# A softmax over sixteen heads: maximum subtracted and rows summed on VectorE, one exponential for four heads on ScalarE

## What is computed

```
def heads(t):                                   # kc = 127 picked tokens, H = 16 heads, hd = 16
    return t.reshape(b, kc, H, hd).transpose(0, 2, 1, 3)
q = rope(heads(hn @ wq), pos_sel)
kk = rope(heads(hn @ wk), pos_sel)
v = heads(hn @ wv)
sc = jnp.einsum('bhqd,bhkd->bhqk', q, kk) / np.sqrt(hd).astype(np.float32)
sc = sc + m_sel[:, None]
a = jax.nn.softmax(sc, axis=-1)
o = jnp.einsum('bhqk,bhkd->bhqd', a, v).transpose(0, 2, 1, 3).reshape(b, kc, d) @ wo
```

## Time and profile before

| what | us |
|---|---|
| median of 3 runs (1541.77 to 1546.73) | 1543.58 |
| the profiled execution: its own time | 1547.94 |
| its span in the trace | 1546.2 |
| TensorE busy in it | 1406.5 (91%) |
| VectorE busy in it | 993.5 (64%) |
| ScalarE busy in it | 693.9 (45%) |

### The profile page before, as it was taken

One profiled execution on the slowest core, in us unless ns is written; L12 is line 12 of the kernel. 1 busy time (PEld: TensorE's weight loads), 2 busy tenths in 40 slices (PEclk: granted clock), 3 DMA queues, 4 the chain that ended last, 5 costly groups with the idle time before them and its releaser, 6 DMA issues.

```text
span 1546.2 us, 23272 instructions
## 1 busy us (share of the span) xinstructions
PE 1406.5 (91%) x8720; PEld 881.4 (57%) x8720; DVE 993.5 (64%) x2776; ACT 693.9 (45%) x1353; POOL 353.1 (23%) x417
## 2 busy tenths in 40 slices
PE   7999999999999999999999999999999999998444
PEld 2447645675457655576446764576555765466333
DVE  2426787377864787377973778647873679737672
ACT  4443544545354552635445353445526354452212
POOL 3004310332104301143103321043111430033210
PEclk9999999999999999999999999999999999999767
DMA  8000010020002001020010200020010200101010
GB/s 292 1 1 29 21 31 22 4 70 28 25 21 73 1 28 38 7 74 20 19 35 3 71 28 25 21 72 2 28 31 14 73 15 15 44 3 44 28 45 4
DMA packets 47536, 54.26 MB, mean 35 GB/s; under 512 B 7608, under 2 KB 42296, under 8 KB 47424
## 3 DMA queue, kind: packets, MB, share of 16 engines
q1 hardware_dynamic: 41408, 46.42, 9.2%
q0 software_dynamic: 6016, 6.35, 1.6%
HBM read 34.84 MB, written 17.87 MB: 34 GB/s over the span
## 4 chain that ended last, share of the span: by engine, by line
PE 81%; DVE 10%; issue 4%; ACT 4%; POOL 1%; DMA 1%; POOLq 0%; DVEq 0%; SPq 0%; ACTq 0%
PE ps L1521 38%; PE ps L1685 7%; PE ps L1595 4%; PE ps L1588 4%; PE ps L1636 3%; PE ps L1825 2%; PE ps L1648 2%; PE ps L1607 2%; PE ps L1835 2%; DVE xT L1192 2%; PE ps L1622 2%; PE ps L1790 2%; PE ps L1613 1%; PE ps L1509 1%; DVE EC L1373 1%
## 5 line engine op out<-in xcount | busy, mean ns | idle before, releaser
L1521 PE MATMUL ps<-xT,wc_s 128*128 128x512 f32 x512 | 232.6, 609 | 0.0
L1521 PE MATMUL ps<-xT,wb_s 128*128 128x512 f32 x512 | 230.9, 597 | 0.1
L1521 PEld LDWEIGHTS ps<-xT,wc_s 128*128 128x128 f32 x512 | 99.7, 198 | 116.5 <-issue 116.2
L1521 PEld LDWEIGHTS ps<-xT,wb_s 128*128 128x128 f32 x512 | 93.6, 190 | 108.4 <-issue 100.9
L1015 DVE SCALAR_TENSOR_TENSOR xT<-xc,cols_s,xT 128x512 f32<-128x512 f32 x192 | 134.9, 749 | 3.2 <-ACT xT L702 0.6
L1685 PE MATMUL ps<-CT,xT 128*128 128x256 f32 x512 | 114.5, 385 | 16.3 <-DVE xT L1192 16.3
L1685 PEld LDWEIGHTS ps<-CT,xT 128*128 128x128 f32 x512 | 98.1, 193 | 35.3 <-issue 21.9
L1521 PE MATMUL ps<-hT,wx_s 128*128 128x512 f32 x256 | 116.4, 604 | 1.3 <-ACT hT L667 1.3
L1521 PE MATMUL ps<-hT,wz_s 128*128 128x512 f32 x256 | 112.3, 592 | 0.0
L734 ACT ACTIVATE BT<-ps 128x512 f32<-128x512 f32 x64 | 37.9, 592 | 155.8 <-PE ps L1521 155.8
L775 ACT ACTIVATE XB<-ps 128x512 f32<-128x512 f32 x64 | 38.4, 599 | 153.6 <-PE ps L1607 153.6
(11 more groups left out here) (297 smaller groups left out, 2625.0 us busy)
## 6 DMA issues: line engine op xcount, KB each, us to landing
BT<-x SPq DMA_DIRECT2D x8, 1024.0 KB, 6.7
xr<-x SPq DMA_DIRECT2D x8, 1024.0 KB, 7.5
x_scratch<-xr SPq DMA_DIRECT2D x32, 256.0 KB, 2.1
out<-EC SPq DMA_DIRECT2D x32, 256.0 KB, 2.1
modrow<-mod_scratch SPq DMA_DIRECT2D x8, 512.0 KB, 4.5
w_s<-w SPq DMA_DIRECT2D x2, 1024.0 KB, 11.6
xT<-wmod SPq DMA_DIRECT2D x1, 1024.0 KB, 8.6
wb_s<-wbT SPq DMA_DIRECT2D x1, 1024.0 KB, 11.4
```

What stands on the lines that cost most here:

```text
L1521: ins = t_.matmul(bank[:, :], w[:, k, m * P:(m + 1) * P], rhs[:, k, half * HALF:(half + 1) * HALF], start=k == 0, stop=k == nk - 1)
```

## The change

The maximum is no longer negated and given to the exponential as a bias: VectorE subtracts it from the 508 columns of a group in place. The exponential is then one instruction for four heads, without bias and without the accumulator. The sums come from a reduction on VectorE at the head of each group in `ffn_probs`. `prob_ready` counts 4 in a batch where it counted 16, and the count of the chain R goes from 44 to 48 for the four new waits of VectorE on itself.

```
-CHAINS = {"A": 4, "V": 9, "D": 7, "S": 3, "G": 20, "R": 44}
+CHAINS = {"A": 4, "V": 9, "D": 7, "S": 3, "G": 20, "R": 48}
...
-        prob_ready = sig("prob_ready", FH)
+        prob_ready = sig("prob_ready", 4)
...
             def ffn_softmax(b):
-                for h in range(FH):
-                    if h % 4 == 0:
-                        act.wait_ge(mx_ready, at(mx_ready, b, h // 4 + 1))
-                    a.activation(scr[:, h, 0:NSEL], scr[:, h, 0:NSEL], ACT.Exp, bias=mx[:, h:h + 1],
-                                 accum_out=den[:, h:h + 1]).then_inc(prob_ready, 1)
+                for r in range(4):
+                    h = slice(4 * r, 4 * r + 4)
+                    act.wait_ge(mx_ready, at(mx_ready, b, r + 1))
+                    a.activation(scr[:, h, 0:NSEL], scr[:, h, 0:NSEL], ACT.Exp).then_inc(prob_ready, 1)
...
                     chR(dve, b, v.tensor_reduce(mx[:, h], scr[:, h, 0:NSEL], AX.X, ALU.max))
-                    v.tensor_scalar(mx[:, h], mx[:, h], -1.0, None, ALU.mult).then_inc(mx_ready, 1)
+                    v.tensor_tensor(scr[:, h, 0:NSEL], scr[:, h, 0:NSEL],
+                                    mx[:, h].unsqueeze(2).broadcast_to([P, 4, NSEL]), ALU.subtract
+                                    ).then_inc(mx_ready, 1)
...
             def ffn_probs(b):
                 for r in range(4):
                     h = slice(4 * r, 4 * r + 4)
-                    dve.wait_ge(prob_ready, at(prob_ready, b, 4 * r + 4))
+                    dve.wait_ge(prob_ready, at(prob_ready, b, r + 1))
+                    chR(dve, b, v.tensor_reduce(den[:, h], scr[:, h, 0:NSEL], AX.X, ALU.add))
                     chR(dve, b, v.reciprocal(den[:, h], den[:, h]))
                     v.tensor_tensor(scr[:, h, 0:NSEL], scr[:, h, 0:NSEL],
                                     den[:, h].unsqueeze(2).broadcast_to([P, 4, NSEL]), ALU.mult
                                     ).then_inc(pn_ready, 1)
```

## The result

The changed kernel takes 1587.27 us (median of 4, 1586.94 to 1589.48) against 1543.86 us of the kernel before in the same runs: a ratio of 1.0277, 95% interval 1.0258 to 1.0297. It is 43.4 us slower; the forecast was 1588.7. The profiled execution took 1587.46, its span is 1585.6.

The account below looks back on a forecast made before the run. TensorE, standing still at the transposes until VectorE ends `ffn_probs`, was taken as the bound. Seven passes of 4.8 + 0.8 us and a last of 4.9 + 1.0 gave 45.1 us, so 1588.7 against the median; range 1573 to 1600.

Parts of the forecast that it names:

- VectorE's queue is the path, and everything added to it arrives: TensorE waits for VectorE ahead of the transposes; each microsecond by which VectorE ends `ffn_probs` later arrives whole in the time.
- a first wait grown by less than 2.5 us: TensorE's wait at the transposes L1790, forecast near 5.9 us; growth below 2.5 us would show the forecast wrong.
- The three further waits: TensorE's waits for the later groups at the transposes, three in each pass, forecast at 0.4 to 0.9 us.
- The first reduction: First group of `ffn_probs`: the new reduction stands behind L1070, starts 0.2 us later, and the group is 2.8 us late.
- The transposes end 4.8 us later: TensorE at L1790: a group every 1.53 us, the last taking 1.19 at low clock, ending at 276.25, 4.8 us late.
- The clock, 0.8 us a pass: L1521 rows behind the transposes: half clock loses 1.95 us, less 1.15 already paid, so 0.8 us more a pass.
- The first rival: TensorE's broken work at the transposes brings the clock up, so the change costs only 26.4 us, 1570; chance 0.10.
- ScalarE at no cost and no gain: Softmax: sixteen exponentials become four, the last ending later at 266.5 but hidden by VectorE's own work; cost nothing.
- The last pass, 5.9 us: Pass without `decay_parts`: L1790 ends 4.9 us late, plus 1.0 us for low clock in the steps behind.
- The sum: Seven passes of 5.6 us, 39.2, plus 4.9 + 1.0: 45.1 us; 1593.0 against the profiled time, 1588.7 against the median.

Follow-up runs that it names:

- the filler ahead: Changed kernel with six extra 128x512 matmuls, results unused, ahead of TensorE's first wait at the transposes in each pass: 1594.20 us, ratio 1.0321.
- the piece put first: Changed kernel with the projection piece that follows the transposes put ahead of them in TensorE's queue: 1578.53 us, ratio 1.0216.
- the second execution of before: The kernel before, without any edit, profiled once more because its first profiled execution lay 4 us above the median: 1540.95 us.
- putting one block ahead of another: Kernel before with `ffn_probs` ahead of `decay_parts` in VectorE's queue: 1514.49 us against 1545.3, ratio 0.9809.

## Why the prediction was right, point by point

*VectorE's queue is the path, and everything added to it arrives.* Right. Subtraction: a group of 2.05 us was forecast and measured, `decay_parts` starts 2.08 us later (forecast 2.1). Normalisation: a period of 1.53 forecast, 1.52 measured.

One sign of a wrong forecast, a first wait grown by less than 2.5 us, came close: the wait grew from 3.05 to 5.57, by 2.52. The three further waits were forecast at 0.4 to 0.9 and are 0.34.

*The first reduction.* Forecast to put the first multiplication 2.8 us late; it is 2.5. The mis-sized step is the 0.2 us for which I let it stand behind the end of `decay_parts`: issued at 267.12, it ends 0.25 us after its predecessor L1069 does (267.50), so most of it was already under way.

*The transposes end 4.8 us later.* Measured 4.54 in the first pass and 4.64 on the average of seven; the group at low clock is 1.19 us, as forecast from the earlier trace rows. Over the seven passes this term is 1 us too large, by the step above.

*The clock, 0.8 us a pass.* Measured in this pair of profiles 0.32 (32.6 us for the seven projection pieces against 30.4). The mechanism is as forecast, and the size wasn't. Over full clock (3.37 us in the timeline) the piece costs 0.97 us more before and 1.29 after, on the average of seven passes, where I had 1.15 and 1.95. I had let the clock come back 4.0 to 6.1 us after the last group starts; it is back after 5.0 us in passes 2, 4 and 6, and after 2.6 in the others, where the piece takes 4.13 us instead of 5.35 and not the 4.8 to 5.9 of the forecast. Here lie 3.4 of the 5.5 us by which the sum exceeded the profiled execution (1593.0 against 1587.46). The first rival, by which the broken work brings the clock up, did not come about: in every pass of the changed kernel the clock is still 0.50 when the last group ends, and in two experiments broken work brings it down by itself (the filler ahead, the piece put first). That the idle stretch is what brings the clock down, as I had reasoned, is only part of it.

*ScalarE at no cost and no gain.* Right: 0.9997 for the fused exponential alone. The Trainium skill, page "VectorE: DVE Perf Modes", section on the TRN2 errata, advises large tiles so that a fixed cost of each instruction is spread. The traces agree: an exponential of 508 columns takes 627 ns, where four of 127 with bias took 1.28 us without the accumulator (the sums alone) and 1.54 with it. The rule says nothing on who waits.

*The last pass, 5.9 us.* Measured from the first scores to the end of the span, it is 6.7 us longer (47.7 against 41.0). The transposes are 4.8 late; the rest is the low clock in the steps behind, of which this timeline of the changed kernel shows the two that matter:

```profile
1552.37 1.19 PE L1792 MATMUL ps<-ident,EC 128*127 128x128 f32 x4 [0.34 <-DVE EC L1388]
...
1554.34 1.94 PE L1805 MATMUL ps<-EC,ftmp 127*32 127x128 f32 x32 [0.78 <-ACT EC L831]
...
1556.86 2.05 PE L1815 MATMUL ps<-fwo_s,ftmp 128*128 128x256 f32 x4 [0.58 <-ACT ftmp L837]
```

*The sum.* Pass by pass and from trace to trace: 34.7 in seven, 6.7 in the last, less 1.4 by which the first scores come earlier and 0.6 between passes, which is 39.4, the difference of the spans. The medians differ by 43.4, because the profiled execution of before lay 4 us above its median. The forecast of 1588.7 came so close to 1587.3 in part by luck: I carried over to the median a sum that is 5.5 us too large for the profiled pair. The extra of the clock is probably larger on the median than in this pair of traces, since the second execution of before, 7.0 us faster, pays less for it than the first. How much larger isn't settled by two profiles.

## What to carry to other kernels

An engine's saved time counts only where somebody waits for it: look for the wait before moving work, and move it away from the engine that carries the chain. Before splitting or fusing, ask for the order in that engine's queue: putting one block ahead of another here gave 31 us, the fused exponential alone nothing. And price what a slower feeder does to TensorE: here the work in pieces, and not the wait ahead of it alone, cost the clock. Filling the wait alone lost 7 us, filling the pieces too gained 13 of the 43. And compare profiles stretch by stretch: differences of 1 to 9 us arose here far from the edit.

## What was unexpected of the hardware

An idle stretch of 5.1 us followed by unbroken transposes cost less clock than one of 3.5 us followed by groups with gaps: the piece behind took 3.5 us in the one (subtraction alone) and 4.9 in the other (sums alone). A low stretch that begins while TensorE still idles is partly free: in the first pass it began 2.6 us ahead of the transposes with the subtraction alone, and 1.5 us behind their start with the sums alone. With the idle stretch filled and the gaps left, the clock still fell, after two or three groups of 0.7 us with 0.9 us between them. In the changed kernel the piece takes 4.13 and 5.35 us in strict alternation from pass to pass; why the low stretch moves by 2.4 us each time is not settled.

And the kernel before, whose idle stretch is 3.04 us, keeps the clock through the transposes in one pass of one execution and in none of another, and has it back before the projection piece in two more. Its runs spread over 8 us (1539.86 to 1548.2), those of the changed kernel over less than 3; that the clock is most of the reason is likely from the two profiles of before, and not shown.
